# Even output tiles by Strassen's block products as well, with their weight sums made on GpSimd and streamed through DRAM

## The reference

```
x1 = x + x @ W.T + bias + (x @ A[id_b].T) @ B[id_b].T      # W 1024 x 1024, A and B of rank 16, one pair a sample
K  = 2 Re( Ct @ exp(dtA * l) )                             # a filter of 1024 taps for each of 64 heads
y  = causal_conv(x1, K) + D * x1                           # along the 1024 features, per head
out = x1 + y * (l < length_b)
```

## Time and profile of the kernel before

| | us |
|---|---|
| median of 3 runs (lowest, highest) | 1107.83 (1107.55, 1108.6) |
| the profiled execution, its own time | 1107.32 |
| its span in the trace | 1105.5 |
| group 0, from the start to the first product of group 1 | 61.45 |
| first matmul of the second stage | 803.48 |

### The profile page before, as it was taken

How to read it: one execution, slowest core, us unless ns; L and a number is a source line. 1 busy time by engine, 2 the same in 40 slices (tenths; PEclk the granted TensorE clock), 3 DMA queues, 4 the chain that set the end, 5 groups by cost and what they waited for, 6 DMA issues and landing times.

```text
span 1105.5 us, 18969 instructions
## 1 busy us (share of the span) xinstructions
PE 1096.8 (99%) x7028; PEld 1005.2 (91%) x7028; DVE 835.0 (76%) x1221; ACT 699.1 (63%) x1180; POOL 27.1 (2%) x79
## 2 busy tenths in 40 slices
PE   8999999999999999999999999999999999999998
PEld 8989998989999998989999898989989999999997
DVE  6987777767777776777777776776468888888886
ACT  5645455555548456455547356455488888888885
POOL 0000000000000000000000000000000000000000
PEclk9999999999999999999999999999999999999999
DMA  7422454434445354444446354445499787879773
GB/s 260 146 79 93 122 175 135 146 134 124 144 134 164 100 179 132 134 135 128 139 134 172 111 169 138 119 147 168 156 301 357 279 343 276 345 275 349 277 281 133
DMA packets 150911, 202.67 MB, mean 183 GB/s; under 512 B 9443, under 2 KB 124324, under 8 KB 147108
## 3 DMA queue, kind: packets, MB, share of 16 engines
q1 hardware_dynamic: 150820, 201.46, 55.3%
HBM read 117.41 MB, written 84.02 MB: 182 GB/s over the span
## 4 chain that ended last, share of the span: by engine, by line
PE 94%; DVE 3%; SPq 1%; issue 1%; DMA 0%; ACT 0%; DVEq 0%
PE acc L1535 30%; PE acc L1710 24%; PE acc L1566 18%; PE acc L1572 9%; PE acc L1518 5%; PE acc L1555 3%; PE acc L1547 3%; PE acc L1745 3%; DVE v_lo L941 1%; DMA w_raw<-w_even 0%; DVE v_raw L977 0%; DVE t_lo L941 0%; PE acc L1654 0%; SPq L393 0%; SPq L397 0%
## 5 line engine op out<-in xcount | busy, mean ns | idle before, releaser
L1535 PE MATMUL acc<-x_hi,w_hi 128*128 128x512 f32 x512 | 200.2, 391 | 1.3 <-DVE w_lo L941 1.3
L1535 PE MATMUL acc<-x_lo,w_hi 128*128 128x512 f32 x512 | 199.9, 390 | 0.0
L1535 PE MATMUL acc<-x_hi,w_lo 128*128 128x512 f32 x512 | 199.5, 390 | 0.0
L1710 PE MATMUL acc<-u_hi,f_hi 128*128 128x512 f32 (+1 forms) x320 | 129.3, 404 | 0.0
L1566 PE MATMUL acc<-t_hi,v_hi 128*128 128x256 f32 x512 | 123.0, 279 | 0.0
L1566 PE MATMUL acc<-t_hi,v_lo 128*128 128x256 f32 x512 | 122.9, 280 | 0.0
L590 ACT ACTIVATE x_sb<-acc,bias_sb 128x512 f32<-128x512 f32 (+1 forms) x128 | 70.1, 575 | 79.9 <-PE acc L1547 62.1
L1710 PE MATMUL acc<-u_lo,f_hi 128*128 128x512 f32 (+1 forms) x320 | 118.5, 370 | 0.0
L1710 PE MATMUL acc<-u_hi,f_lo 128*128 128x512 f32 (+1 forms) x320 | 118.5, 370 | 0.0
L1535 PEld LDWEIGHTS acc<-x_hi,w_lo 128*128 128x128 f32 x512 | 96.2, 188 | 20.6
L1535 PEld LDWEIGHTS acc<-x_hi,w_hi 128*128 128x128 f32 x512 | 96.1, 188 | 19.8 <-DVE w_lo L941 1.7
(11 more groups left out here) (202 smaller groups left out, 2506.7 us busy)
## 6 DMA issues: line engine op xcount, KB each, us to landing
x_scratch<-x_sb SPq DMA_DIRECT2D x32, 1024.0 KB, 5.4
out<-out_sb SPq DMA_DIRECT2D x63, 512.0 KB, 4.5
x_raw<-x_t SPq DMA_DIRECT2D x15, 2048.0 KB, 9.1
u_raw<-x_scratch SPq DMA_DIRECT2D x14, 2048.0 KB, 11.8
wq_raw<-state_scratch SPq DMA_DIRECT2D x16, 1024.0 KB, 8.0
a_raw<-lora_a SPq DMA_DIRECT2D x128, 64.0 KB, 1.9
b_raw<-lora_b SPq DMA_DIRECT2D x128, 64.0 KB, 2.8
state_scratch<-g_sb SPq DMA_DIRECT2D x16, 512.0 KB, 3.2
```

The costliest lines, as they stand in the source:

```text
L1535: mm = pe.matmul(acc[:, o_bank(g, i), :], w, m, start=k == 0 and s == 0, stop=False)
L1710: mm = pe.matmul(bank, w, m, start=first and i == 0, stop=last and i == 2, skip_group_check=onto_closed)
```

## The change

What it does:

- From group 1 on, the even tiles are computed by seven block products too (`p = 0`; the odd tiles are `p = 1`). TensorE's order in a group becomes p1, p1, adapters_down, (filters), p2, p2, p6, p6, end_11 twice, p3, p3, p7, p7, end_12 twice, then p5, p4, end_22, end_21 of the even tiles and the same of the odd ones. The banks of PSUM rotate among A, B and C of each half. Group 0 keeps the plain even tiles (`plain_tile`).
- The even tiles' weights don't fit in SBUF in seven versions. S2 and S3 are kept; the high and low parts of A11, A12, S4, S1, A22 are in DRAM (5 x 1 MB) and are loaded through two slots, five loads a group on SyncE.
- The even sums are made once by GpSimd in groups 0 and 1: ten additions and, after ScalarE's high parts, four subtractions, each of 128 x 1024. A part is wanted as hi + lo, so that the sums have up to four terms.
- In group 0 weights come in four pieces beside the pieces of `x`, and the first two tiles advance together, k by k. The exponential of `log_dt` (`filter_steps_per_head`) moves from group 0 to group 1.
- On SyncE, `load_b` now stands ahead of the store of the odd result, and the loads of the weights stand among the adapters' and `x` loads. On ScalarE, `even_out` is gone from the groups, and the seeds and outs stand twice.
- The number of warming matmuls falls from 24 to 14. In the second stage one ScalarE order changes around heads 0 and 1, and which buffers the first heads use.

The diff, cut to its core:

```diff
-    w_hi = place("w_hi", [P, HALF, NT, P], F32R)
-    w_lo = place("w_lo", [P, HALF, NT, P], F32R)
+    SLOTS = 4
+    w_pair = place("w_pair", [P, SLOTS, 2, HALF, QT, P], F32R)
-    A_BANK, D_BANK, B_BANK, C_BANK, O_BANK, H_BANK, E_BANK = 0, 1, 2, 3, 4, 6, 7
+    H_BANK, D_BANK = 6, 7
+    TRIO = ((4, 5, 0), (2, 1, 3))
-    SPINS = 24
+    SPINS = 14
+    STREAM = (A11, A12, S4, S1, A22)
+    KEPT = {S3: 2, S2: 3}
...
+            def load_ws(g, j):
+                n = stream_of(g, j)
+                if n < 2:
+                    return
+                used, count = {A11: (m_p5, g - 1), A12: (m_p4, g - 1), S4: (m_p1, g), S1: (m_p2, g), A22: (m_p3, g)}[j]
+                sp.wait_ge(used[0], count)
+                sp.wait_ge(st_ws[STREAM.index(j)], 32 if j in (S4, S1) else 16)
+                sp.dma_start(r32(w_pair[:, n % 2, :, :, :, :]).rearrange("p s k i n -> p (s k i n)"),
+                             ws_d[STREAM.index(j)].rearrange("p s k n -> p (s k n)")).then_inc(ld_ws[n % 2], 16)
...
+            for g in range(1, n_groups):
+                sp.wait_ge(st_x1[0], 16 * g)
+                for i, row in enumerate(rows):
+                    load_b(i, row)
+                store_x1(g - 1, 1)
+                if g == 1:
+                    sp.wait_ge(c_elo, 3)
+                    store_sum(S4)
+                load_ws(g, S4)
+                if g == 1:
+                    sp.wait_ge(c_elo, 4)
+                    store_sum(S1)
                 if g < LAST:
                     rows = [adapter_of(g + 1, i) for i in range(G)]
                     sp.wait_ge(c_alo, 2 * (g + 1))
+                    sp.wait_ge(st_x1[1], 16 * g)
                     for i, row in enumerate(rows):
                         load_a(i, row)
+                load_ws(g, S1)
...
                 filter_stores(g, 0)
                 if g < LAST:
                     load_x(g + 1)
+                load_ws(g, A22)
                 filter_stores(g, 1)
...
+                if g < LAST:
+                    load_ws(g + 1, A11)
+                    load_ws(g + 1, A12)
+                    store_x1(g, 0)
+                    filter_stores(g, 2)
+                    continue
...
             for g in range(1, n_groups):
-                out_21(g - 1)
-                seed_b(g)
+                out_21(1, g - 1)
+                seed_b(0, g)
                 split_t(g, "T2")
+                seed_b(1, g)
                 split_b(g)
                 take_h(g)
                 split_h(g)
+                if g == 1:
+                    split_even(S1)
                 split_t(g, "T3")
                 if g < LAST:
                     split_a(g + 1)
-                even_out(g, 0)
                 filter_step(g, 0)
-                seed_c(g)
-                out_11(g)
+                seed_c(0, g)
+                seed_c(1, g)
+                out_11(0, g)
                 split_t(g, "T1")
-                even_out(g, 1)
+                out_11(1, g)
                 filter_step(g, 1)
+                seed_e(0, g)
+                seed_e(1, g)
+                split_t(g, "T4")
                 if g < LAST:
-                    for t in range(NT):
+                    for t in range(HALF):
+                        split_x(g + 1, t)
+                    take_p5(0, g)
+                    for t in range(HALF, NT):
                         split_x(g + 1, t)
                 else:
+                    split_filter(0)
+                    split_u_early(0)
+                    take_p5(0, g)
+                    split_filter(1)
+                    split_u_early(1)
+                out_21(0, g)
...
+            def even_sums():
+                pool.wait_ge(c_w0lo, W0_PARTS)
+                pool.wait_ge(c_wlo, 2)
+                add_up(s1, a21, a22, ALU.add)
+                add_up(s1, s1, a21_lo, ALU.add)
+                add_up(s1, s1, a22_lo, ALU.add)
+                add_up(part, a11, a21, ALU.subtract)
+                add_up(part, part, a11_lo, ALU.add)
+                pool.wait_ge(m_plain, 1)
+                add_up(s3, part, a21_lo, ALU.subtract)
+                pool.wait_ge(st_ws[STREAM.index(A22)], 16)
+                add_up(s2, s1, a11, ALU.subtract)
+                add_up(s2, s2, a11_lo, ALU.subtract)
+                add_up(s4, a12, s2, ALU.subtract)
+                add_up(s4, s4, a12_lo, ALU.add)
...
             for g in range(1, n_groups):
-                p1(g)
+                for p in range(2):
+                    p1(p, g)
                 adapters_down(g)
-                even_base(g, 0)
                 filters(g)
-                p2(g)
-                even_base(g, 1)
-                even_adapters(g, 0)
-                p6(g)
...
+                for p in range(2):
+                    p2(p, g)
+                for p in range(2):
+                    p6(p, g)
+                for p in range(2):
+                    end_11(p, g)
+                for p in range(2):
+                    p3(p, g)
+                for p in range(2):
+                    p7(p, g)
+                for p in range(2):
+                    end_12(p, g)
+                for p in range(2):
+                    p5(p, g)
+                    p4(p, g)
+                    end_22(p, g)
+                    end_21(p, g)
```

More of the change, by code:

```diff
@@ L427, in load_zb @@
                     sp.wait_ge(st_z, 16)
+                    sp.wait_ge(st_ws[STREAM.index(S1)], 32)
                 else:
@@ L918, in _ @@
                 split_states(h, 0, 2)
+                if h > 0 and ahead:
+                    split_filter(h + 2)
+                take_state(h, 2)
+                split_states(h, 2, 3)
                 if h == 0:
@@ L1539, in even_adapters, with plain_products, first_tiles @@
-            def even_adapters(g, i):
-                if i == 0:
+            def plain_products(i, k):
+                r, ii = divmod(i, QT)
+                c, kk = divmod(k, HALF)
+                pairs = products([w_pair[:, 2 * r + c, s, kk, ii, :] for s in range(2)], (x_hi[:, k, :], x_lo[:, k, :]))
+                for s, (w, m) in enumerate(pairs):
+                    mm = pe.matmul(acc[:, plain_bank(i), :], w, m, start=k == 0 and s == 0, stop=False)
+                return mm
+            def first_tiles():
+                for k in range(NT):
+                    if k % 2 == 0:
+                        pe.wait_ge(c_w0lo, k // 2 + 1)
+                    pe.wait_ge(c_xlo, k + 1)
+                    for i in range(QT):
+                        plain_products(i, k)
@@ new lines, in plain_tile, with plain_adapters @@
+            def plain_tile(i):
+                for k in range(NT):
+                    if k % HALF == 0:
+                        pe.wait_ge(c_wlo, k // HALF + 1)
+                    mm = plain_products(i, k)
+                return mm
+            def plain_adapters(i):
+                if i == 0:
+                    pe.wait_ge(c_blo, 2)
+                    pe.wait_ge(c_hlo, 2)
+                    pe.wait_ge(c_hhi, 2)
+                for c in range(2):
+                    for s, m in enumerate((hh, hl)):
+                        mm = pe.matmul(half(acc[:, plain_bank(i), :], c), b_st[:, c, 2 * i, :], half(m[:, :], c),
+                                       start=False, stop=c == 1 and s == 1)
+                mm.then_inc(m_even, 1)
@@ new lines, in adapters_up, with weights @@
+            def adapters_up(p, bank, r, c):
+                for i in range(QT):
+                    for s, m in enumerate((hh, hl)):
+                        mm = pe.matmul(by_row(bank_part(bank, i)), b_st[:, c, tile_of(p, r, i), :], half(m[:, :], c),
+                                       start=False, stop=s == 1, skip_group_check=True)
+                return mm
+            def weights(p, g, j):
+                if p == 1:
+                    if g == 0:
+                        pe.wait_ge(c_vlo, v_order.index(j) + 1)
+                    return v_hi[:, j, :, :, :], v_lo[:, j, :, :, :]
+                if j in KEPT:
+                    if g == 1:
+                        pe.wait_ge(c_elo, 1 if j == S2 else 2)
+                    slot = KEPT[j]
+                else:
+                    n = stream_of(g, j)
+                    if n >= 2:
+                        pe.wait_ge(ld_ws[n % 2], stream_loads(n))
+                    slot = n % 2
+                return w_pair[:, slot, 0, :, :, :], w_pair[:, slot, 1, :, :, :]
```

744 lines of the change are left out of this document (394 added, 350 removed).

## The result

| | before | after |
|---|---|---|
| median (lowest, highest), us | 1107.71 (1107.55, 1108.6), 4 runs | 1185.12 (1182.85, 1188.34), 4 runs |
| ratio, 95% interval | | 1.0699 (1.0671 to 1.0728) |
| profiled execution, its span, us | 1107.32, 1105.5 | 1188.34, 1186.6 |
| first product of group 1 | 61.28 | 84.01 |
| first matmul of the second stage | 803.31 | 884.19 |

The kernel became 7% slower; the forecast was 1082 us, 2.3% faster. The profiled execution lies 3 us above the median. The last two rows are read from TensorE's timelines; the 61.45 and 803.48 given further up for the kernel before lie 0.17 us late, both alike. The spans differ by 81.1 us: 22.7 at the start, 58.2 in the 15 groups (800.2 against 742.0 us), 0.2 in the second stage.

A forecast was written before the change was run, and what follows sets the result against it. TensorE was taken to bound the groups through matmul count times start distance, VectorE's chain group 0. 1107.3 - 31.5 (products) + 7 (seeds) - 3.5 (start) + 3 (handover) = 1082.3, forecast 1082 us, range 1072 to 1106.

The forecast's parts named there:

- GpSimd. Cost zero in the forecast.: Even weights' sums on GpSimd: 2.2 us each, done in time, disturbing nobody, so 0 us.
- rival (b): Group 0: GpSimd and VectorE take turns, A11's low part at 56.8, total 1104 us; chance 0.25.
- -3.5 us: Group 0: new order of pieces and moved exponential end it at 57.9 instead of 61.45; between 0 and -6.
- A at 17: Groups: the adapters' A is there 17 us into the group, after the odd store and index reads.
- 1.5 us late: Groups with a filter step before p3: seed_c(0) ready at 23.1, needed at 21.6.
- Forecast +7, bound +21: Seed waits before p3 in seven groups: +7 us in all; +21 if A comes at 19.8, 3 us each.
- some 7 us before: Even weights' start: S4 and S1, stored and reloaded, are back some 7 us before p3 and p5 need them.
- The handover: Last group: odd p5 waits for take_p5(0), behind the split of late u; +3 us (0 to 6).
- the three verdicts: Whole kernel against the one before: faster 0.79, same 0.07, slower 0.14.
- (c): Groups: weight stream late at 210 GB/s, p4 waits 3.4 us for A22 in each of 15; 1133 us, chance 0.10.
- (d): Both GpSimd and VectorE taking turns and A as late as before: 1118 us, chance 0.07.
- The matmuls' arithmetic: 15 groups: seven block products replace four plain even tiles, 46.9 us a group instead of 49.0; -31.5 us in all.

The follow-up runs named there:

- E3: Changed kernel with GpSimd's ten sums and four low parts replaced by memsets that read nothing, values left out: 1167.31 us.
- E9: Kernel before the change plus ten unused GpSimd additions of 128x1024 in group 0: 1125.72 us, ratio 1.0161.
- E10: Changed kernel with 15 unused 512-column matmuls between end_11 and p3 in seven groups with a filter step: 1172.17 us.
- E1: Changed kernel with seed_c of both halves ahead of split_a and filter_step on ScalarE: 1160.93 us, ratio 1.0479.
- E7: E6 with ScalarE's take_p5(0) ahead of splitting the first filters and u in the last group: 1144.15 us, ratio 1.0329.
- E6: E5 with ScalarE's second filter step moved behind the last bank's seeds and T4's high part: 1145.83 us.
- E12: E7 with GpSimd's sums and subtractions as memsets and no weight loads from group 2 on, values left out: 1109.57 us, ratio 1.0022.
- E4: Changed kernel without the five weight loads a group from group 2 on, even tiles' values left out: 1148.94 us.
- E5: E1 with the load of A22 issued ahead of the next x on SyncE: 1161.16 us.
- E13: E7 with GpSimd's ten sums held back until the low part of A11's odd weights is made: 1146.72 us.
- E14: E9 with the additions held back until VectorE has made the low parts of all seven odd weights: 1130.35 us, ratio 1.0202.

## Why the prediction was wrong

**The failing steps**, by what they cost against the sum:

- *"GpSimd. Cost zero in the forecast."* It was rival (b), to which I gave 0.25. It said A11's low part at 56.8 and group 1 near 79; it was 54.95 and 84.01. I rested on GpSimd's 64 small instructions that keep 400 ns, and had noted in the same breath that they fall into holes of VectorE: they could not speak against it. I also priced an addition at 2.2 us; it took 2.5 to 3.3. Group 1 started 26.1 us behind the forecast of 57.9. Memsets (E3) take 18.8 of it away, as E9 adds 18.2; the other 7.3 (65.17 against 57.9) say that the term "-3.5 us" for the new order of pieces was wrong in sign as well: 61.28 became 65.17. In E3 A11's low part came at 38.29, where the term has 35.4 and the kernel before 36.84; VectorE's list didn't start earlier, it waited 2.0 us for ScalarE's part of `h_own`.
- *"A at 17"*, and so "1.5 us late". In group 10 the odd store was issued 6.1 us into the group instead of 5 and landed 6.7 us later instead of 6, another 1.7 us that stood in no term lie between its landing and the first load of A, and A was split at 20.4. That is as late as before, my upper bound. The bound of 3 us a group was mis-sized by its own ruler: with A at 19.8 instead of 17 the seed is 1.5 + 2.8 = 4.3 us late. A plus the filter step gave holes of 3.5 to 5.9, and three groups without a step there waited too, up to 2.4. Forecast +7, bound +21; measured 39 us in groups 2 to 13.
- *The halved clock* behind a hole stood in no term. It was 2.35 us for the one read closely, 13 us by E10 for seven holes, and by the clock's records 26 us beside 62 us of holes in the groups.
- *Groups 1 and 2* stood in no term. p3 of group 1 waited 10.5 us for its seed, which stood behind the split of A, whose loads stood on SyncE behind the store of S1: A's way was worked out for a common group alone. S4 was back in time, as I had it; S1, which I had "some 7 us before" need as well, was 1.2 us late with the seeds first (E1), and A22, queued behind it, 7.8. Group 2 waited 4.2 us for A11.
- *The handover*: +3 forecast, 7.8 measured. With the order changed (E7) a hole of 5.4 us for `u` is left where E6 had 6.7, so it was `u` that was mis-sized: its two loads landed after 11.7 and 15.7 us, where they took 7.9 each before.
- *The chances of the three verdicts* don't add up as written: (c) and (d) alone are 0.17, where "slower" has 0.14. The forecast doesn't hang on it.

**The right steps.** The matmuls' arithmetic: 46.9 us in the groups of E12 without a hole, and the product's 1.88 + 0.94 us unchanged. The second stage kept its 302 us. The stream did run at 228 GB/s; TensorE didn't wait for A22 in the kernel after, as I had it when I turned down rival (c), but the stream's price (36 us by E4, one run) came through the odd store, A behind it, and `u`. I had costed its own five transfers and left the others' durations as they were before.

**What sums up.** Against the kernel before, 81 us: 22.7 at the start, 62 of holes in the groups, 26 of halved clock, 0.2 in the second stage, less the 31.5 that the products do save. That makes 79.4; the other 1.7 us aren't assigned.

## What to carry to other kernels

A stage in which TensorE has no slack but the others seem to have a quarter is bound by the order of their lists, not by their busy share: for each added wait, work out the new time of its input with the transfers as long as the new traffic makes them, and price each hole at its length plus the slower clock that may follow it. Work put on GpSimd isn't free for a kernel whose VectorE is a link in the chain: count GpSimd's whole time as VectorE's, unless it only writes, as in E3, or VectorE is idle then. None of the five places tried here hid it. And when a hole closes, look who waits in its place: E1, E4, E5, E7 and E13 each lost a part of a gain, or all of it, to the input that was second latest.

## What the runs showed of the hardware

- **GpSimd and VectorE take turns by whole instructions.** A two-input VectorE instruction of 128x1024 rose from 1.22 to 3.4 us, one of 128 columns from 0.28 to 2.46, one of 64 columns from 0.22 to 2.4. An addition on GpSimd took 2.4 us in E14, beside short instructions, and up to 3.3 in the kernel after, beside long ones. Not touched were the one with one input in PSUM (0.68 us at 36.45, while the next, with both in SBUF, took 2.05) and the one beside two memsets (1.23 us at 37.06 in E3). The Trainium skill ("SBUF — State Buffer", Who interferes with whom) states that a VectorE instruction with two SBUF inputs contends with a GpSimd instruction that reads SBUF, not with one that only writes; all of these rows agree. It also says that a tensor_scalar can contend, when it enters one of its two-port modes: of three in a row in E14 two took 2.38 and 2.21 us, the one between them, which writes int32, 0.20. Which mode they ran in no trace shows.
- **The clock falls in a hole.** Behind the one of 4.7 us, in which TensorE did nothing, the granted clock was 0.50 (1.2 GHz), and it was back in the window from 598 to 601 (0.73); behind what E10's filling matmuls left of the same group's hole, 2.33 us, it stayed at 1.00. A hole's length alone doesn't settle it: in the kernel after, the clock stayed at 1.00 over the 3 us behind group 2's hole of 2.44 us and was 0.68 behind group 7's of 2.35.
- **More traffic lengthened some transfers and not others.** With the stream, the traffic in the groups went from 139 to 228 GB/s, and the stores of x1 took 6.4 us instead of 5.4 at the median. The 64 KB loads of A kept their 1.9 us, and the 2 MB loads of `x` took 7.8 us instead of 9.1 (7.7 without the stream, E4); why these came sooner no run shows.
